# Graph attention: the first and last two blocks of each half are visited head by head

## The reference, cut to what matters

```
h = (x @ W).reshape(N, H, C)                                  # N = 3125, H = 4, C = 32
logits = leaky_relu(a_src[src] + a_dst[dst], 0.2)
m = segment_max(logits, dst);  e = exp(logits - m[dst])
s = segment_sum(e, dst);       alpha = e / s[dst]
out = segment_sum(h[src] * alpha[:, :, None], dst)
```

## Time and profile before

| | us |
|---|---|
| median of 3 runs | 3396.24 |
| lowest and highest | 3393.32, 3400.12 |
| the profiled execution | 3386.61 |
| its span in the trace | 3384.8 |
| VectorE busy | 2239.6 (66%) |
| TensorE busy | 2711.3 (80%) |
| ScalarE busy | 1681.8 (50%) |

### The profile page before, as it was taken

How to read it: one execution, slowest core, us unless ns; L and a number is a source line. 1 busy time by engine, 2 the same in 40 slices (tenths; PEclk the granted TensorE clock), 3 DMA queues, 4 the chain that set the end, 5 groups by cost and what they waited for, 6 DMA issues and landing times. The chain is left out here.

```text
span 3384.8 us, 62842 instructions
## 1 busy us (share of the span) xinstructions
PE 2711.3 (80%) x21373; PEld 2260.9 (67%) x21373; DVE 2239.6 (66%) x4934; ACT 1681.8 (50%) x2854; POOL 202.9 (6%) x481
## 2 busy tenths in 40 slices
PE   2777877553448888788856999899997999979997
PEld 1555555342346666566645998879996999869997
DVE  8988988631439999899976555545555555455555
ACT  1656565420228888788854444444444444434433
POOL 1000000000000000000000111011110111011110
PEclk9989898876669999899978999999998999989999
DMA  2798888976043324433302333133331333223331
GB/s 52 148 180 162 173 158 171 178 168 162 0 134 115 107 106 137 145 115 115 112 27 86 114 113 124 49 117 125 120 116 42 132 113 115 76 97 113 113 124 47
DMA packets 204514, 389.72 MB, mean 115 GB/s; under 512 B 164475, under 2 KB 176563, under 8 KB 180693
## 3 DMA queue, kind: packets, MB, share of 16 engines
q1 hardware_dynamic: 204343, 387.48, 41.0%
HBM read 286.12 MB, written 100.30 MB: 114 GB/s over the span
## 5 line engine op out<-in xcount | busy, mean ns | idle before, releaser
L1712 DVE CUSTOM_DVE_ANT_0 l_arow<-l_scores,abias 125x500 f32<-125x500 f32 (+1 forms) x525 | 325.4, 621 | 366.7 <-issue 313.1
L1648 PE MATMUL l_asum<-vals,l_awcol 125*125 125x129 f32 x3750 | 516.2, 277 | 31.4 <-DVE l_awcol L1042 28.2
L1648 PEld LDWEIGHTS l_asum<-vals,l_awcol 125*125 125x125 f32 x3750 | 454.6, 187 | 58.5 <-DVE l_awcol L1042 49.8
L1301 PE MATMUL gturned<-ident,grow 125*125 125x125 f32 x2500 | 408.4, 305 | 27.5 <-ACT grow L1241 27.5
L1301 PEld LDWEIGHTS gturned<-ident,grow 125*125 125x125 f32 x2500 | 331.3, 204 | 104.9 <-issue 73.0
L1210 DVE SCALAR_TENSOR_TENSOR grow<-line,a_dst 125x3125 f32<-125x3125 f32 x100 | 347.5, 3475 | 47.6 <-DMA line<-lines_dram 40.4
L1040 ACT ACTIVATE l_awcol<-l_aturned 125x500 f32<-125x500 f32 (+1 forms) x225 | 122.7, 546 | 510.9 <-PE l_aturned L1657 510.9
L1683 ACT ACTIVATE l_arow<-l_arow,l_aneg 125x500 f32<-125x500 f32 (+1 forms) x525 | 323.6, 659 | 82.6 <-DVE l_aneg L1718 82.6
L1241 ACT ACTIVATE grow<-grow,neg 125x3125 f32<-125x3125 f32 x100 | 290.3, 2903 | 130.4 <-DVE neg L1222 130.4
L1219 DVE CUSTOM_DVE_ANT_0 grow<-grow,bias 125x3125 f32<-125x3125 f32 x100 | 341.6, 3416 | 15.0 <-DMA bias<-bias_dram 0.8
L1279 PE MATMUL gparts<-gwcol,h_mem 125*32 125x125 f32 x5000 | 242.7, 289 | 119.1 <-ACT gwcol L1254 119.1
(11 more groups left out here) (324 smaller groups left out, 4451.7 us busy)
## 6 DMA issues: line engine op xcount, KB each, us to landing
abias<-bias_dram SPq DMA_DIRECT2D x100, 1562.5 KB, 6.5
bias<-bias_dram SPq DMA_DIRECT2D x50, 1562.5 KB, 6.5
counts_dram<-blk SPq DMA_DIRECT2D x37, 1367.2 KB
bias_dram<-lnrow SPq DMA_DIRECT2D x25, 1562.5 KB, 6.9
counts<-counts_dram SPq DMA_DIRECT2D x25, 683.6 KB
line<-lines_dram SPq DMA_DIRECT2D x8, 1367.2 KB
counts_dram<-blk SPq DMA_DIRECT2D x37, 158.7 KB
fixed<-kp SPq DMA_DIRECT2D x250, 4.0 KB, 4.4
```

The source lines that it names most:

```text
L1301: last = pe.transpose(bank[q % RING][:, j // 4, j % 4 * T:(j % 4 + 1) * T], row[n % RING][:, t * T:(t + 1) * T], ident[0:T, 0:T])
L1648: last = pe.matmul(sum_ps[p][:, :], wcol[c % T_BANKS][:, j * T:(j + 1) * T], vals[:, t, :], start=(t == 0), stop=(t == NT - 1))
L1712: dve.tensor_tensor_reduce(out=row[p][:, a:z], in0=s_ps[c % S_BANKS][:, 0:z - a], in1=bias[p][0:T, a:z], scale=1.0, scalar=-3.0e38, op0=AL ...
```

## The change

The order of visits is now a list. In each half the first two blocks are taken together, and the last two: first both blocks with g = 0, then both with g = 1. The blocks between them are visited as before. For half 0 the order is (block, head) = (0,0) (1,0) (0,1) (1,1) (2,0) (2,1) ... (22,0) (22,1) (23,0) (24,0) (23,1) (24,1), and the same follows for half 1.

The waits go by the place of a visit in the list (`after`). The line of half 1 for g now waits for the logits of block 24 with that head: visit 47 for g = 0, visit 49 for g = 1. A bias tile i waits for the maximum of block i - 2 with g = 1. SyncE's order becomes line 0, bias 0, bias 1, line 1, bias 2, ..., bias 24, line 0 of half 1, bias 25, line 1 of half 1, bias 26, and so on. The copies of the sums take two heads at once only where two neighbouring visits of a set are the two heads of one block; otherwise one head each.

```diff
+            order = [(b, g) for two in ((0, 1), *((b,) for b in range(2, NT - 2)), (NT - 2, NT - 1)) for g in range(2) for b in two]
+            visits = [(half, b, g) for half in range(2) for b, g in order]
+            after = {v: n + 1 for n, v in enumerate(visits)}
             def unit(n):
-                half, b, g = n // (2 * NT), n // 2 % NT, n % 2
+                half, b, g = visits[n]
                 return half, b, g, 2 * half + g
...
                         if half:
-                            sp.wait_ge(logits_made, 2 * NT * half - 1 + g)
+                            sp.wait_ge(logits_made, after[half - 1, NT - 1, g])
...
                         if i >= 2:
-                            sp.wait_ge(max_done, 2 * (i - 2) + 2)
+                            sp.wait_ge(max_done, after[(i - 2) // NT, (i - 2) % NT, 1])
...
                     load_lines(0, 0)
                     load_bias(0)
+                    load_bias(1)
                     load_lines(0, 1)
-                    for i in range(1, 2 * NT):
+                    for i in range(2, NT):
                         load_bias(i)
-                        if i == NT:
-                            for g in range(2):
-                                load_lines(1, g)
+                    load_lines(1, 0)
+                    load_bias(NT)
+                    load_lines(1, 1)
+                    for i in range(NT + 1, 2 * NT):
+                        load_bias(i)
...
                     def maximum(n):
                         half, b, g, k = unit(n)
-                        i = n // 2
+                        i = half * NT + b
...
-                            for g in range(SET // 2):
-                                half, b, _, k = unit(SET * u + 2 * g)
-                                last = act.activation(sums[:, b, k:k + 2, :], sum_ps[:, 2 * g:2 * g + 2, :], ACT.Copy)
+                            e = 0
+                            while e < SET:
+                                half, b, g, k = unit(SET * u + e)
+                                wide = 2 if e + 1 < SET and unit(SET * u + e + 1) == (half, b, g + 1, k + 1) else 1
+                                last = act.activation(sums[:, b, k:k + wide, :], sum_ps[:, e:e + wide, :], ACT.Copy)
+                                e += wide
                             last.then_inc(sum_copied, 1)
```

More of the change, by code:

```diff
@@ L1259, in _ @@
                             u = (n - 1) // SET - 1
-                            half, b, g, k = unit(SET * u)
                             act.wait_ge(sum_ready, u + 1)
-                            for g in range(SET // 2):
-                                half, b, _, k = unit(SET * u + 2 * g)
-                                last = act.activation(sums[:, b, k:k + 2, :], sum_ps[:, 2 * g:2 * g + 2, :], ACT.Copy)
+                            e = 0
[4 more added lines that the diff above has]
+                                e += wide
                             last.then_inc(sum_copied, 1)
```

## The result

| | before | after |
|---|---|---|
| median of 6 runs, us | 3395.32 | 3378.99 |
| lowest and highest | 3390.45, 3400.12 | 3377.59, 3393.58 |
| the profiled execution's span | 3384.8 | 3376.5 |

The ratio is 0.996, with a 95% interval of 0.9941 to 0.9979: 7 to 20 us faster, 13.6 by the ratio. The prediction was 9.0 us saved (a ratio of 0.9973), which lies in both intervals.

What follows compares the result with a forecast made beforehand. VectorE sets the stage, and the DMA queue bounds its waits for lines at the start and middle. The terms -3.7 - 5.5 + 0.2 = -9.0 us give 3387.2 us, range 3381 to 3394, with 2 in 10 outside.

Steps and rivals of the forecast that it cites:

- The queue bounds both places, and what is saved there stays saved: At the start of each half the DMA queue causes VectorE's 40.4 us of line waits; savings there last to the end.
- The start, 3.7 us: Start of half 0: visit 1 runs before the second line lands, so the logits of visit 2 start 3.7 us earlier.
- The middle, 5.5 us, between 3.8 and 6.2: Change of halves: line 0 reloads earlier, bias 26 lands earlier, saving 5.5 us, with bounds 3.8 and 6.2.
- the shortest pieces of the forecast (37.2): Middle queue: shortest times for line, bias, line, bias, 15.7 + 3.5 + 14.5 + 3.5 = 37.2 us, giving 6.2 us saved.
- The pairs at the end of half 1 and the copies: Visits 96 to 99 gain nothing from order; two extra ScalarE copies in the last set cost 0.24 us (0 to 0.44).
- The forecast's list of loads issued one visit nearer to their use: Biases 2, 24 and 27, issued later than before, all have at least 10.9 us of cover against 6.5 to 6.8.
- TensorE's waits stay at nine, give or take 2 us: VectorE's 0.8 us waits for TensorE stay nine; two or three more or fewer, 2 us, go into the range.
- the sign given for being wrong: The forecast would be wrong if VectorE's waits for TensorE numbered more than some twelve.
- the second rival: Three to seven more 0.8 us TensorE waits leave 3.4 to 6.6 us saved, about 3391; chance 0.20, including run scatter.
- Lines at the rate of bias tiles: Rival: lines move like two bias tiles (7 us); start saves 3.7, middle about 0, 3.5 in all, 3392.7; chance 0.06.
- TensorE stays slow after the wait: Rival: TensorE keeps the low clock after the longer middle wait; five such visits make +7.5 us, 3404; chance 0.04.
- No effect: Rival: the order does nothing because VectorE is the bound anyway, 3396 us; chance 0.02.

Runs made afterwards that it cites:

- the second profile: The changed kernel measured and profiled again with no edit, against the kernel before: ratio 0.9977, 7.8 us faster.
- a fourth row: The changed kernel with four row buffers for VectorE's logits instead of three, against the kernel before: ratio 0.9958, 14.2 us faster.
- the last comparison: Separate measurement of two four-row kernels, one reordered with an added wait (0.9924), one otherwise unchanged (0.9982), against the kernel before, which took 3364 us there.
- bias 26 first, four rows: Changed kernel with bias 26 ahead of half 1's second line, no pair at half 1's end, four row buffers; against the kernel before: 0.9956, 14.9 us faster.
- the same with one wait more: "bias 26 first, four rows" plus one VectorE wait at visit 3 for something long done; against the kernel before: 0.9924, some 25 us faster.
- the start pair alone: The kernel before with only blocks 0 and 1 of half 0 taken together and bias 1 ahead of the second line: 0.9982, 6.1 us faster.

## Why the prediction was right, step by step

- *The queue bounds both places, and what is saved there stays saved.* Right, as far as TensorE lets it: in the first profile 4.3 of the 9.2 us saved were lost again to its waits. Undoing the order of loads turned the change into a loss of 8.5 us with the same visits.
- *The start, 3.7 us.* Right in mechanism, low in size: 4.9 and 4.5 us in the two profiles. The term that was off is the landing of the second line: it was taken 37.9 us after the first issue and was there after 36.7 (964.66 to 1001.37), and after 37.0 in the second profile.
- *The middle, 5.5 us, between 3.8 and 6.2.* 4.3 and 6.7 us. In the first profile the four transfers took 39.1 us, near the 39.6 of the middle before rather than the 37.9 of the start; in the second they took 36.7, less than the shortest pieces of the forecast (37.2). That 5.5 lies between the two is right in the mean and not in either. A wait of 0.79 us for TensorE at visit 48 cost nothing there, nor did one of 2.06 us in the second profile, since they fall before the wait for bias 26. The prediction did not see that the two pairs of the middle do different things. The one at the end of half 0, which lets the line be reloaded one visit earlier, carries the saving (3.6 us alone); the one at the start of half 1 saves nothing alone. That it is needed once bias 26 goes ahead of the second line follows from the order, since the second visit of the half would otherwise wait for that line; no run has bias 26 first without it.
- *The pairs at the end of half 1 and the copies.* Nothing to be had, and 0.13 us more for the last four copies, where 0.24 was forecast. (The forecast's list of loads issued one visit nearer to their use leaves out bias 49, which was not waited for either.)
- *TensorE's waits stay at nine, give or take 2 us.* This is the step that was mis-sized: 11.2 and 16.0 us in the two profiles against 7.2 before, 4.0 and 8.8 more. The number, 11 and 12, is at the edge of the sign given for being wrong ("more than some twelve"); what the forecast did not have is the single wait of 2 us, since the profile of before has only waits of 0.8. It is the second rival, and it does eat part of the saving in single executions. It did not overturn the forecast of the medians; a possible reason, not shown, is that the other executions of the kernel before have such waits too, as other orders do (14.7 and 13.3 us with one pair, but 7.2 with another). Whether the change makes them more frequent isn't settled; with a fourth row they can't matter.
- *Lines at the rate of bias tiles*: excluded. (The forecast's argument, 14.5 to 15.2 us "four times", counts too many: its rows show two lines at that, and the first one at 15.7.) The middle would then have saved nothing, and the queue of four still took 39.1 us. (By the 341 GB/s of the Trainium skill, DMA: Bandwidth & Descriptors, Bandwidth, its 9.5 MB would take 28 us, as an estimate; the measurement decides.)
- *TensorE stays slow after the wait*: not seen to last. After visit 52 the first wait for it is at visit 68, at 1492.70; in the second profile it is one of 0.77 us at visit 60.
- *No effect*: by the times alone the change is small, but both intervals lie below 1.

That a load moved ahead in SyncE's order lands ahead is shown by the old order of loads against the new. The Trainium skill (DMA: Bandwidth & Descriptors, Queues, rings and completion order) says that each DMA engine takes a ring's descriptors in order, and warns that completion is not in order for DMAs spread over different numbers of engines; in all runs here these large loads landed in the order of their issue, in agreement with the first part.

## What to carry to other kernels

When a loop stands still for loads at its ends, list the loads in their order in the queue with the landing times, and ask of each what the first work is that needs it: here the new order of work paid only with a new order of loads, and otherwise the wait just moved to the next buffer in the same queue. A buffer's reload can start a whole visit earlier if its last use is pulled forward, which cost the engines no more than a few small copies here. And compare a stage by the distance between its instructions, for several profiles: here what lay ahead of the stage moved by 9 us between executions (first logits at 977.8 to 987.0 us, the last comparison left aside), as much as the effect.

## What was not expected of the hardware

- One wait more or less in VectorE's straight code changed the time of a loop that comes much later by some 7 us: 1645.2 to 1647.1 us behind the stage in three profiles without it, 1637.8 to 1640.3 in nine with it, with 102 and 72 waits of TensorE for the same copy. The place of the later code is the likely cause, since nothing else differs between "bias 26 first, four rows" and the same with one wait more; through what it acts (fetching, or the loop's branch) no run shows. The count of instruction transfers behind the stage does not tell them apart: 12 in one queue and 8 or 9 in another in all four kernels with four rows.
- TensorE at the low clock (0.5) can make VectorE wait 2 us at a time, at several ends of sets one after another (2.13, 2.08, 2.05 and 2.03 us at visits 20, 24, 28 and 32 with the start pair alone). In a stretch of ten microseconds that ends shortly before each of them the clock was 0.50 to 0.53 with TensorE busy 9.8 to 10.0. Before waits of 0.8 us it was 0.66, low for part of the time (kernel before, 1098 to 1108 us), and ahead of visit 36 of the start pair alone, which has no wait, it was 1.00 with TensorE busy 9.5.
- Two lines and two bias tiles do not always take the same time. At the start, in the order line, bias, bias, line, it was 36.7 to 38.0 us from the first issue to the last landing in seven profiles. In the middle, in the order line, bias, line, bias, it was 39.1 and 36.7 us in the two profiles of the changed kernel and 39.9 with four rows. What makes the difference stays open. The end of the queue is not full either: in the last 3.9 us before visit 2 of the changed kernel the DMA share was 0.38, and in the last 1.8 us before bias 26 was there it was 0.05.
